# Graph attention on one core: products with v behind the first stretch of projections, ScalarE storing all q/k units, and GpSimd issuing the stores of y and the loads of x

## The reference, cut to what matters

```
h = relu(layernorm(x))                       # x: 64 batches of 128 rows by 384
q, k, v = h@Wq+bq, h@Wk+bk, h@Wv+bv          # 12 heads of 32
scores = q k^T / sqrt(32) + beta*adj         # only where adj > 0, else -9e15
out = x + softmax(scores) v                  # per batch and head, adj: 128 x 128
```

## Time and profile before

| | before |
|---|---|
| median of 3 runs (lowest, highest) | 549.69 us (548.75, 551.79) |
| the profiled execution's own time | 552.24 us |
| its span | 550.4 us |
| PE busy | 504.8 us, 92% |
| DVE busy | 469.1 us, 85% |
| ACT busy | 443.3 us, 81% |
| POOL busy | 127.4 us, 23% |
| mean granted TensorE clock | 0.991 of full speed |
| transfers | 106.19 MB, 59.6% of the 16 DMA engines |

### The profile page before, as it was taken

The page is one execution under the profiler, slowest core; times in us unless marked ns, Lnnn a source line. Parts: engine busy times, 40 slices in busy tenths (PEclk is TensorE's granted clock), DMA queues, the critical chain, the costliest instruction groups (busy, mean ns, idle before and its releaser), DMA issues.

```text
span 550.4 us, 17259 instructions
## 1 busy us (share of the span) xinstructions
PE 504.8 (92%) x5142; PEld 417.6 (76%) x5142; DVE 469.1 (85%) x2323; ACT 443.3 (81%) x1816; POOL 127.4 (23%) x204
## 2 busy tenths in 40 slices
PE   8998897887999989899998989989898999999986
PEld 7776776765887878688787878868786887888774
DVE  5687697967899899889989989889997998887796
ACT  3567687786697969879796997879798797989885
POOL 5411021212122222212222222222222221111131
PEclk9999999999899999989999999999999999999999
DMA  8424465656577667767766775776667566644311
GB/s 256 155 88 153 132 222 164 214 194 210 168 231 232 222 214 231 231 184 231 233 221 219 239 226 174 234 234 221 219 230 233 172 197 213 193 154 149 107 59 58
DMA packets 111959, 106.19 MB, mean 193 GB/s; under 512 B 12448, under 2 KB 97312, under 8 KB 111904
## 3 DMA queue, kind: packets, MB, share of 16 engines
q1 hardware_dynamic: 111904, 105.56, 59.6%
HBM read 55.84 MB, written 49.68 MB: 192 GB/s over the span
## 4 chain that ended last, share of the span: by engine, by line
SPq 30%; DMA 27%; PE 18%; DVE 8%; issue 7%; ACT 1%; DVEq 0%
DMA out_rows<-out_blocks 14%; SPq L425 12%; DMA probs_rows<-probs_blocks 10%; SPq L454 7%; PE G_ps L906 7%; SPq L401 6%; PE S_ps L975 4%; SPq L416 3%; DMA probs_moved<-probs_rows 3%; PE S_ps L927 2%; DVE probs L737 2%; PE PT_ps L959 2%; PE PT_ps L943 2%; SPq L393 1%; ACT probs L538 1%
## 5 line engine op out<-in xcount | busy, mean ns | idle before, releaser
L538 ACT ACTIVATE probs<-probs,negmax 128x128 f32<-128x128 f32 x532 | 206.1, 397 | 0.0
L737 DVE CUSTOM_DVE_ANT_0 probs<-S_ps,bias 128x128 f32<-128x128 f32 x768 | 166.1, 285 | 17.7 <-PE S_ps L927 17.4
L553 ACT ACTIVATE probs_blocks<-probs,negmax 128x128 f32<-128x128 f32 x236 | 92.0, 392 | 77.2 <-DVE negmax L737 67.1
L509 POOL TENSOR_TENSOR w_raw<-w_raw,x_ring 128x384 f32<-128x384 f32 x63 | 64.0, 1017 | 312.7 <-DVE w_raw L757 312.7
L906 PE MATMUL G_ps<-h_hi,w_hi 128*128 128x512 f32 x288 | 119.6, 415 | 0.0
L906 PE MATMUL G_ps<-h_hi,w_lo 128*128 128x512 f32 x288 | 118.6, 412 | 0.0
L906 PE MATMUL G_ps<-h_lo,w_hi 128*128 128x512 f32 x288 | 117.2, 407 | 0.0
L538 ACT ACTIVATION_READ_ACCUMULATOR probs<-probs,negmax 128x1 f32 x532 | 104.9, 197 | 0.0
L927 PEld LDWEIGHTS S_ps<-qk 32*128 32x128 f32 x1536 | 50.9, 189 | 38.0 <-issue 36.6
L927 PE MATMUL S_ps<-qk 32*128 32x128 f32 x1536 | 63.7, 294 | 15.7 <-DVE h_lo L676 10.4
L943 PE MATMUL PT_ps<-probsT,v 128*32 128x128 f32 x1512 | 54.7, 277 | 20.2 <-DVE probsT L778 13.9
(11 more groups left out here) (60 smaller groups left out, 725.6 us busy)
## 6 DMA issues: line engine op xcount, KB each, us to landing
probs_rows<-probs_blocks SPq DMA_DIRECT2D x59, 256.0 KB, 3.1
probs_moved<-probs_rows SPq DMA_DIRECT2D x236, 64.0 KB, 2.0
out_dram<-w_raw SPq DMA_DIRECT2D x63, 192.0 KB, 2.9
x_ring<-in_x_dram SPq DMA_DIRECT2D x61, 192.0 KB, 2.8
out_rows<-out_blocks SPq DMA_DIRECT2D x29, 384.0 KB, 3.3
w_raw<-out_rows SPq DMA_DIRECT2D x116, 96.0 KB, 2.2
xhat_rows<-xhat_blocks SPq DMA_DIRECT2D x26, 384.0 KB, 2.5
xhat_moved<-xhat_rows SPq DMA_DIRECT2D x104, 96.0 KB, 2.7
```

The lines of the kernel that those rows point to most:

```text
L509: nc.gpsimd.tensor_tensor(y[:, place, :], y[:, place, :], x_ring[:, bass.ds(at, D)], ALU.add).then_inc(y_ready, 1)
L538: last = nc.scalar.activation(p, p, ACT.Exp, bias=negmax[:, e, j * KC + m:j * KC + m + 1], scale=TURN, accum_out=rowsum[:, e, m * HC + j:m ...
L553: last = nc.scalar.activation(blocks[:, j, :, :], probs[:, a, j, 0, :].rearrange("p (c e) -> p c e", c=HC), ACT.Exp, bias=negmax[:, a, j * ...
L737: last = nc.vector.tensor_tensor_reduce(probs[:, a, j, m, :], S_ps[:, j, m * N:(m + 1) * N], bias[(z.par + 1) % 2][:, z.s, :], 1.0, LARGES ...
```

## The change

PE: `scores` comes first in every slot, `probs_times_v` stands behind `STRETCH_1`, and in slot 3 ("closing") `STRETCH_2` stands ahead of `values`. VectorE: the mask comes first in every slot; `add_bv` moves behind `mask_terms` (in slot 3 to behind `low_part`); `quotient` and then `transpose_probs` become the last of the slot; the store of unit 5 is gone. ScalarE stores unit 5 too (`STORE_Q`), behind `high_part`, which now stands ahead of the copies of the transposed probabilities. SyncE reads `out_rows` a slot later, at the head of an even slot, behind the reads of `probs_rows`; the reads of `xhat_rows` are spread over two slots (`READS`). GpSimd stores y right behind its addition and loads x at the end of its slot.

```diff
-LOADS = [[0], [1], [2, 3], []]
+LOADS = [[0], [1, 2], [3], []]
+READS = [[0, 1], [2, 3], [0, 1], [2, 3]]
-STORE_V = [[], [], [], [5]]
+STORE_Q = [[], [], [], [5]]
...
# SyncE
+                if z.W and z.s % 2 == 0 and z.pairs_before or z.first_f:
+                    sp.wait_ge(out_rows_written, 16 * z.pairs_written())
+                    for b in range(HC):
...
+                        sp.dma_start(goes, came).then_inc(out_blocks_moved[z.s // 2], 16)
...
-                for d in z.moved + z.turned:
-
-                    sp.wait_ge(y_ready, z.o + 1 - d)
-                    place = (z.s - 2 - d) % GROUP
-                    sp.dma_start(out[bass.ds(z.o - d, 1), :, :].rearrange("b t d -> t (b d)"), y[:, place, :]).then_inc(out_written[place], 16)
...
# GpSimd
+                    pool.wait_ge(y_ready, z.o + 1 - d)
+                    nc.gpsimd.dma_start(out[bass.ds(z.o - d, 1), :, :].rearrange("b t d -> t (b d)"), y[:, place, :]).then_inc(out_written[place], 16)
                 for q in z.stats:
                     deviation(q, z.place(q)[0])
+                if not (z.static and z.groups(3) >= NG):
...
+                    for q in LOADS[z.s]:
+                        nc.gpsimd.dma_start(x_ring[:, bass.ds(z.ring(3, q), D)],
...
# ScalarE
                 if z.Q:
                     exponentials_ahead(z)
+                if z.M:
+                    high_part(z)
+                if z.P:
+                    for u in STORE_Q[z.s]:
+                        store_qk(z, u)
...
# VectorE
+                if z.A:
                     mask(z)
                 if z.O:
                     store_outT(z)
...
+                        if z.A and not z.closing:
+                            add_bv(z)
                     statistics(q, s)
...
+                if z.A and z.closing:
+                    add_bv(z)
+                if not z.F:
+                    for d in z.moved:
+                        quotient(z, d)
+                if z.R:
+                    transpose_probs(z)
...
# TensorE
+                if z.A:
+                    scores(z)
                 if z.P:
                     for part in STRETCH_1[z.s]:
                         project(z, *part)
+                if z.O:
+                    probs_times_v(z)
+                if z.closing:
+                    for part in STRETCH_2[z.s]:
+                        project(z, *part)
                 if z.A:
                     values(z)
```

More of the change, by code:

```diff
@@ L409, in load_ahead @@
                                  adj_v[:, bass.ds(z.groups(1), 1), :, :].rearrange("q g s k -> q (g s) k")).then_inc(adj_loaded[(z.par + 1) % 2], 16)
[L410 to L417, removed]
             def slot(z):
@@ L425, in slot @@
                         sp.dma_start(goes, came).then_inc(probs_blocks_moved[(z.s - 1) % 2], 16)
-                load_ahead(z)
[L427 to L433, removed]
+                if z.W and z.s % 2 == 0 and z.pairs_before or z.first_f:
+                    sp.wait_ge(out_rows_written, 16 * z.pairs_written())
+                    for b in range(HC):
+                        came = out_rows[z.s // 2, :, b * SIX:(b + 1) * SIX].rearrange("(j p) n -> p j n", j=HC)
+                        goes = out_moved[b * HD:(b + 1) * HD, z.s // 2, :].rearrange("p (j n) -> p j n", j=HC)
+                        sp.dma_start(goes, came).then_inc(out_blocks_moved[z.s // 2], 16)
+                load_ahead(z)
+                xhat_here = not (z.static and not 1 <= z.groups(0) <= NG - 3)
+                if xhat_here and z.s == 2:
+                    sp.wait_ge(rows_written[0], 16 * z.groups(0))
+                if xhat_here and z.s >= 2:
+                    read_blocks(0, READS[z.s])
                 if z.M and z.s == 0:
                     sp.wait_ge(rows_written[1], 16 * z.groups(-1))
-                    read_blocks(1)
+                if z.M and z.s < 2:
+                    read_blocks(1, READS[z.s])
+                if xhat_here and z.s % 2 == 1:
+                    sp.wait_ge(xhat_ready, order(z.count(2)) + 1)
+                    write_rows(z.s // 2)
                 if z.W and z.s % 2 == 1:
@@ L617, in slot @@
                     store_probsT(z, 2)
-                if z.M:
-                    high_part(z)
                 if z.P:
-                    for u in STORE_2[z.s] + STORE_V[z.s] * (z.static and z.groups(0) == 0):
+                    for u in STORE_2[z.s]:
                         store_qk(z, u)
@@ L813, in slot @@
                     return
-                if z.F and z.A:
-                    mask(z)
                 if z.O and not z.F:
                     reciprocals(z)
-                if z.scores_first:
+                if z.A:
                     mask(z)
@@ L821, in slot @@
                     store_outT(z)
-                if z.A and not z.F and not z.scores_first:
-                    mask(z)
                 if z.M:
@@ L829, in slot @@
                     reciprocals(z)
-                for d in z.moved:
-                    quotient(z, d)
-                if z.A:
+                if z.F:
+                    for d in z.moved:
+                        quotient(z, d)
+                if z.F and z.A:
                     add_bv(z)
-                if z.R:
-                    transpose_probs(z)
                 if z.F and z.A:
@@ L872, in slot @@
                     normalise(z, q)
-                if z.P and not first:
-                    for u in STORE_V[z.s]:
-                        store_qk(z, u)
+                if z.A and z.closing:
+                    add_bv(z)
+                if not z.F:
+                    for d in z.moved:
+                        quotient(z, d)
+                if z.R:
+                    transpose_probs(z)
                 if first and z.s == GROUP - 1:
@@ L1027, in slot @@
                         warm(WARM[GROUP])
-                if z.A and z.scores_first:
-                    scores(z)
-                if z.O:
-                    probs_times_v(z)
-                if z.A and not z.scores_first:
+                if z.A:
                     scores(z)
@@ L1044, in slot @@
                     transpose_probs(z, 2)
-                if z.P:
+                if z.P and not z.closing:
                     for part in STRETCH_2[z.s]:
```

66 lines of the change are left out of this document (23 added, 43 removed).

## The result

The changed kernel takes 587.49 us (median of 4 runs, 585.07 to 588.7) where the kernel before takes 549.22 in the same comparison: a ratio of 1.069, 95% interval 1.063 to 1.075. The forecast was 537 us and the range ended at 557. The profiled execution of after took 585.07 us, its span is 583.2, its mean granted clock 0.961.

What follows compares the result with a forecast made beforehand. PE was taken to bound the kernel, SyncE's ring just above it. Groups 5 to 13 −3.5, groups 2 to 4 −10.5, group 14 +1.1, group 15 −0.5, first loads +0.5: −12.9 us, forecast 537 us, range 523 to 557.

Steps and rivals of the forecast that it cites:

- The floor: PE, per group: two slots of 7.55 us with 14 projection products, two of 7.31 with 13, together 29.7 us.
- SyncE, the step that failed: SyncE's reads of `out_rows` at the head of an even slot: last lands at 7.35 us, so `quotient` waits 0.3.
- VectorE: VectorE's slot: transpose ends near 8.5 us, before the next mask at 8.75; PE's 13.9 us of waits gone.
- path B: GpSimd's last load of x lands late; `moments` waits 1.9 us in slot 3, and the next scores start 1.9 late.
- Groups 2 to 4: Early groups: two thirds of their 13.9 us excess go, 4.6 stay; 99.4 us, a change of −10.5.
- Path A: PE, slot 3: `values` behind 13 products delays the low part and `add_bv`, costing 1.0 us a group.
- ScalarE: ScalarE's one more store per group: costed at nothing, or 0.6 us a group should its cover go.
- Rival 1: GpSimd's issue is cheap, 0.43 us, so groups take 30.7 us: 521 us in all; chance 0.15.
- Rival 2: Load of x later still, `moments` waits at slot 3, kernel slower: 564 us, or 555; chance 0.22.
- g: Price of one transfer issue on GpSimd: between 0.43 and 1.77 us, taken as 1.03.
- Rival 3: GpSimd's issue stands behind a VectorE instruction, making it 1.58 us: 550 us, no change; chance 0.13.
- Rival 4: SyncE's ring still rules, 30.8 us a group, 32.0 with slower landings: 542 us; small form within the forecast's 0.50.

Runs made afterwards that it cites:

- the run with the early products: Changed kernel with `out_rows` reads in the odd slot, x loaded in slots 0 and 1, and products with v back right behind the scores: ratio 1.024.
- the issue alone: Kernel before, in its own order on all engines, with only the stores of y and loads of x issued by GpSimd: 546.8 us, ratio 0.989.
- the repaired kernel: Changed kernel with two edits, reads of `out_rows` back in the odd slot and all x loaded in slots 0 and 1: 547.5 us, ratio 0.989.

## Why the prediction was wrong

*The bound and the floor.* Right that PE with a ring behind it is the bound. The floor of 29.7 us a group was taken from the old order and carried over; in the new one the products with v are enclosed by other kinds on both sides, a slot is 0.21 us longer (the run with the early products has 7.55 and 7.32 again), and the floor is 30.6. That is 0.84 in 13 groups, 11 us that no term of the sum held.

*SyncE, the step that failed.* "The last of these landing 2.2 after its issue at 5.15", that is at 7.35, so that the quotient, which could start at 7.07, "waits 0.3". The issues were right to 0.2 (3.62 and 5.37 against 3.8 and 5.6). The landing was not: 4.0 us in slot 2 where I had put the median of before, with GpSimd's two loads, issued at 297.90, in flight. With x on SyncE behind the reads they land in 2.3. With GpSimd's loads issued 3 us ahead of them (loads one slot earlier) it is 2.5. It is not the place in the slot: in the issue alone reads issued at 1.67 of slot 2, with two loads beside them, take 3.5 at the median, and near the end of after, when no x is left to load, reads issued at 4.08 of slot 2 (475.15) take 2.2. The Trainium skill, "DMA: Bandwidth & Descriptors", section "Issuing engines are not separate DMA queues", says that transfers of all engines run on the same 16 DMA engines and interleave; the rows agree, and I had priced the landing as if they did not. Worse than the number was its use: I saw a slack of −0.3 us, wrote it off, and went on. The reads of `out_rows` back in the odd slot are worth 6.4 points. That run is also the nearest to what I had drawn, a quotient that hardly waits: its span is 551.1 us, 13.6 above my 537.5, and 11 of these are the floor.

*VectorE.* "Nothing of this is on PE's path in slots 0 to 2." The transpose is indeed in time there, and PE's 13.9 us are gone. Without its wait the quotient would have started at 7.00 (9.08 − 2.08), where 7.07 was drawn. But its lateness has a way that I had drawn myself for path B, through GpSimd to the load, and I fed it 0.3.

*Path B.* The mechanism is the one described: 12 waits for x, one in the start and 11 at slot 3, these of 2.1 us on average. Its parts: the quotient 1.7 us later than drawn (9.08 against 7.37); the addition as drawn; the issue of a transfer 0.58 us instead of 1.03, but 0.69 of waiting for GpSimd's own sum before y's, which the sum had not; `deviation` 1.0; load to `moments` 2.35 behind the end of its issue, against 2.4. The three prices of GpSimd nearly cancel (the load is issued by 13.70, and 12.22 + 1.71 is 13.93), so the later quotient is the whole of it. Slot 2 being 0.21 longer, x lands 1.2 later in slot 3 than drawn, and the stall is 3.1 us where 1.9 stood. The 0.4 us more by the first bytes stated in the Trainium skill, "DMA: Bandwidth & Descriptors", section "Latency and other measured facts", did not show at this place: from the end of the issue to `moments` it is 2.35 where the sum had 2.4.

*What the stall set off.* The clock at half speed for some 6 us behind nine of twelve stalls was in no term. It is 1.55 us in the group above and at least 1.4 points in all. So the 35.27 us of that group are my 31.6, 0.84 of floor, 1.3 of longer stall and 1.55 of clock. The longer stall goes back to the landing, and the clock to the stall.

*Groups 2 to 4.* I let two thirds of their excess of 13.9 go; they take 110.7 us instead of 109.9. Three groups of 35.02 are 105.1, so 5.6 us of excess stay (I had 4.6), under a steady group that is dearer.

*The sum.* Groups 5 to 13 missed by 30.8 (315.1 against 284.4), groups 2 to 4 by 11.3, group 14 by 1.2, start and end by 2.5: 45.7, the distance from 537.5 to 583.2.

*Path A* was right: 1.14 to 1.21 with everything else repaired.

*ScalarE* cost nothing: in no row of after is the store of unit 5 what PE waits for longest. In the repaired kernel it comes near: the weight loads of the scores wait for it 12.6 us in 9 places, and v is later still.

*The rivals.* Rival 1 had the price of the issue nearly right (0.58) and the time wrong, since that price was not what ruled. Rival 2 had the right place, the wait of `moments` at slot 3, and the right sign, but its lever was g, with g = 1.57 as the point from which it decides; the lever was the start of the quotient, which enters the same chain one for one. Rival 3 is not borne out: the 63 stores of y are issued in 0.557 to 0.608 us, beside a VectorE that is busy for 78% of the span. Rival 4 had the ring, and in the run with both issues on SyncE the ring does rule (1.057). It also let each landing take 0.3 us more, but carried that into SyncE's ring alone. None of the four let the quotient move; the one that reached past 557, rival 2 with 564, did so by the price of the issue, and the range ended at 557.

## What to carry to other kernels

An instruction put last in a slot takes over the lateness of whatever it waits for, and hands it to everything that hangs on its result: follow it to the end of that chain, on every engine, before its wait is called free. Price a landing by the transfers that the change will put beside it, not by the median of the kernel before, and treat a slack of a few tenths as none; the room for the reads was worth 6.4 points here. Issuing from an idle engine wins (1.1% in the old order, 1.6 points with both edits and the early products) as long as no load that others need stands in its queue behind a late wait.

## What the runs showed of the hardware that I had not expected

- GpSimd issues a 192 KB transfer in 0.58 us (0.557 to 0.608 over 63 stores); SyncE takes 0.38 at the median for the loads of x in before and 0.43 for the stores of y.
- Between the end of its own addition and the issue that waits for it GpSimd stands 0.69 us in the row shown, 34.1 us over 62 times, 0.7 at the longest.
- A load of x issued by GpSimd lands in 3.3 us at the median, 2.8 when SyncE issues it; a set of four reads of `out_rows` takes 2.2 to 2.4 us at the median without them, and took 3.5 and 4.0 in the two sets above with two of GpSimd's loads issued within half a microsecond of the first.
- With the products with v between two kinds of projection a slot takes PE 0.21 us more than with them behind the scores (7.76 against 7.55).
- Behind a stall of 3.09 us PE ran at the lower of its two clocks for some 6 us, behind three others of 2.93 to 3.35 it did not; with short products in the stall the clock stayed at 1.00 for the whole span.
